# A decoder layer on one core: self scores from three fp32r products of parts, and cross keys and values ahead of the projections of x

## The reference

```
def reference(x, ctx_1024, mask, ...):
    x = x + self_attn(layernorm(x))                  # 16 heads of 64, softmax over queries (axis -2)
    x = x + cross_attn(layernorm(x), ctx_1024, mask)  # 16 heads of 8, 512 keys
    x = x + ffn(layernorm(x))                        # 8 experts, top 2, and a shared one
    return x

# self_attn
q, k, v = (split_heads(x @ W + b, 16) for W, b in ((Wq, bq), (Wk, bk), (Wv, bv)))
pattern = einsum('bhid,bhjd->bhij', k, q) / 8
prob = softmax(pattern, axis=-2)
out = einsum('bhis,bhid->bhsd', prob, v)
```

## Time and profile before

| | us |
|---|---|
| median of 3 runs | 206.96 |
| lowest and highest run | 206.8, 211.75 |
| profiled execution | 206.72 |
| its span, first to last instruction | 204.9 |
| PE busy in the span | 194.9 (95%) |
| DVE, ACT, POOL busy | 153.0, 132.2, 97.2 |

### The profile page before, as it was taken

One profiled execution on the slowest core, in us unless ns is written; L12 is line 12 of the kernel. 1 busy time (PEld: TensorE's weight loads), 2 busy tenths in 40 slices (PEclk: granted clock), 3 DMA queues, 4 the chain that ended last, 5 costly groups with the idle time before them and its releaser, 6 DMA issues.

```text
span 204.9 us, 4417 instructions
## 1 busy us (share of the span) xinstructions
PE 194.9 (95%) x1562; PEld 151.7 (74%) x1562; DVE 153.0 (75%) x409; ACT 132.2 (65%) x308; POOL 97.2 (47%) x145
## 2 busy tenths in 40 slices
PE   7899998999999899996999999999989999999995
PEld 7588876678777667863756656676658799999994
DVE  2576787577559788579999999999983867458844
ACT  2475458697679649279998898987985332462220
POOL 7599107757673787905759991002400017500330
PEclk9999999999999999999999999999999999999999
DMA  6970477989734402324004200000000000000001
GB/s 174 386 198 3 154 102 93 100 102 134 89 53 126 134 2 77 79 82 153 0 4 122 31 3 0 2 3 2 0 3 0 3 0 5 0 0 16 0 0 38
DMA packets 10980, 12.67 MB, mean 62 GB/s; under 512 B 984, under 2 KB 8920, under 8 KB 10888
## 3 DMA queue, kind: packets, MB, share of 16 engines
q1 hardware_dynamic: 9856, 11.15, 26.8%
q10 hardware_dynamic: 1008, 1.06, 1.6%
q0 software_dynamic: 96, 0.20, 0.6%
HBM read 10.96 MB, written 1.44 MB: 61 GB/s over the span
## 4 chain that ended last, share of the span: by engine, by line
PE 69%; DVE 10%; ACT 9%; issue 4%; POOL 3%; DMA 3%; ACTq 0%; DVEq 0%; POOLq 0%
PE ps L938 13%; PE ps L899 8%; PE ps L962 8%; PE ps L825 7%; PE ps L841 6%; PE ps L714 6%; PE ps L797 5%; PE ps L876 5%; PE ps L858 4%; ACT q_t L631 3%; PE ps L727 3%; DMA biases<-in_biases 3%; ACT prob L597 3%; PE ps L916 2%; DVE q_t L1164 2%
## 5 line engine op out<-in xcount | busy, mean ns | idle before, releaser
L1164 DVE CUSTOM_DVE_ANT_0 q_t<-ps,mask_add 128x512 f32<-128x512 f32 x64 | 41.3, 682 | 3.3 <-PE ps L858 2.0
L486 POOL TENSOR_TENSOR prob<-prob,rec 128x512 f32<-128x512 f32 x32 | 32.4, 1040 | 23.5 <-DVE rec L1223 23.5
L597 ACT ACTIVATE prob<-ps,low 128x256 f32<-128x256 f32 x64 | 29.7, 490 | 10.5 <-DVE low L1154 10.5
L631 ACT ACTIVATE q_t<-q_t,low 128x512 f32<-128x512 f32 x44 | 29.3, 717 | 4.2 <-DVE low L1164 4.1
L1154 DVE TENSOR_REDUCE low<-ps 128x2 f32<-128x512 f32 x32 | 20.4, 682 | 8.5 <-PE ps L797 8.5
L899 PEld LDWEIGHTS ps<-ident,q_t 128*128 128x128 f32 x176 | 19.6, 141 | 8.7 <-ACT q_t L631 2.9
L522 POOL TENSOR_TENSOR place_k<-place_k 128x256 f32<-128x256 f32 x10 | 7.3, 732 | 38.8 <-DVE place_k L1189 38.8
L899 PE MATMUL ps<-ident,q_t 128*128 128x128 f32 x176 | 23.7, 276 | 2.1 <-ACT place_k L667 0.8
L617 ACT ACTIVATE q_t<-ps 128x512 f32<-128x512 f32 x18 | 10.6, 598 | 21.1 <-PE ps L938 21.1
L1210 DVE TENSOR_TENSOR q_t<-q_t,ps 128x512 f32<-128x512 f32 x18 | 12.2, 684 | 11.8 <-PE ps L938 7.0
L841 PE MATMUL ps<-ident,prob 128*128 128x128 f32 x128 | 18.4, 278 | 1.4 <-POOL prob L486 0.9
(11 more groups left out here) (173 smaller groups left out, 428.9 us busy)
## 6 DMA issues: line engine op xcount, KB each, us to landing
k_stack<-k_dram SPq DMA_DIRECT2D x9, 256.0 KB
wg<-in_L_ffn_w_gate SPq DMA_DIRECT2D x1, 1024.0 KB, 23.6
wu<-in_L_ffn_w_up SPq DMA_DIRECT2D x1, 1024.0 KB, 35.0
q_stack<-q_dram SPq DMA_DIRECT2D x6, 144.0 KB
k_dram<-prob SPq DMA_DIRECT2D x1, 768.0 KB, 3.6
w_in<-in_L_attn_Wq ACTq DMA_DIRECT2D x2, 256.0 KB, 5.6
context<-in_ctx SPq DMA_DIRECT2D x1, 512.0 KB, 5.7
w_in<-in_L_attn_Wv SPq DMA_DIRECT2D x1, 512.0 KB, 7.5
```

Of the source, the lines that this page charges most:

```text
L486: nc.gpsimd.tensor_tensor(pr, pr, rec1[:, s % 2, r, :].unsqueeze(2).to_broadcast([P, C, S]), ALU.mult).then_inc(s_norm1, 1)
L597: e = nc.scalar.activation(prob1[:, s % 3, r, c * S:(c + 1) * S], ps[:, 2 * (s % 2) + r, c * S:(c + 1) * S], ACT.Exp, bias=low1[:, s % 2, ...
L631: nc.scalar.activation(prob2[n % 3][:, c, :], score2[n % 2][:, c, :], ACT.Exp, bias=low2[:, n % 2, c:c + 1], scale=-1.0).then_inc(s_exp2, 1)
L1164: nc.vector.tensor_tensor_reduce(out=score2[n % 2][:, c, :], in0=ps[:, 2 * (n % 2) + c, :], in1=mask_add[:, c, :], scale=1.0, scalar=3e38, ...
```

## The change

*Parts.* For each item of q and k ACT now writes the high part with its bias (fp32r, `q1_high`, `k1_high`, in the places of `q1_t` and `k1_t` and what follows), and DVE, after it, the low part from the same bank into `qk1_low`. The scale of -1/8 moves from the evacuation of q into the parts of Wq. The scores are three products for each head, with the two heads in turn. `qk1_low` lies where `k2_stack` will lie, which is why the loads of the stack now wait for the scores of their batch row and are made for one batch row at a time.

*Prologue.* Cross keys and values come first in the list of items, around the transposed x; transfers are issued in another order and the context in two halves; the mask moves into the first cycle; 12 matmuls on the identity stand at the start instead of 17.

```diff
-    out = [("x_t", 0, "dve"), ("kx", 0, "act"), ("kx", 1, "act")]
+    out = [("kx", 0, "act"), ("x_t", 0, "dve"), ("kx", 1, "act"), ("vx", 0, "act"), ("vx", 1, "act")]
     for p in range(NP):
-        out += [("q", p, "act"), ("k", p, "dve")]
-        if p == 2:
-            out += [("vx", 0, "act"), ("vx", 1, "act")]
+        out += [("q", p, "dve"), ("k", p, "dve")]
...
         @block.sync
             load(x_in[:, 0:C, :], a["x"][:, 0:C, :], d_x)
+            load(ctx_t[:, 0:BANK], a["ctx_1024"][:, 0:BANK], d_ctx[0])
             load(wk1[:, 0:BANK], a["L0_attn_Wk"][:, 0:BANK], d_qk[1][0])
-            load(ctx_t, a["ctx_1024"], d_ctx)
-            load(wk2[:, :], a["L0_xattn_Wk"], d_wk2)
             load(wv2[:, :], a["L0_xattn_Wv"], d_wv2)
+            load(wk1[:, BANK:2 * BANK], a["L0_attn_Wk"][:, BANK:2 * BANK], d_qk[1][1])
...
-            sp.wait_ge(d_kdram, 16)
-            for j in range(PARTS):
-                for i in range(PARTS):
-                    r = (j * PARTS + i) * HD2
-                    load(k2_stack[r:r + HD2, :, :], k2_dram[j].rearrange("(d h) t -> d h t", d=HD2), d_kstack)
+            def stack_keys(b):
+                sp.wait_ge(d_kdram, 16)
+                sp.wait_ge(s_score1, 2 * NP * (b + 1))
+                for j in range(PARTS):
+                    for i in range(PARTS):
+                        r = (j * PARTS + i) * HD2
+                        load(k2_stack[r:r + HD2, b, :, :],
+                             k2_dram[j, :, b * SK:(b + 1) * SK].rearrange("(d h) t -> d h t", d=HD2), d_kstack[b])
...
+            stack_keys(0)
             for b in range(B):
                 sp.wait_ge(s_qparts, b + 1)
...
                 if b == 0:
+                    stack_keys(1)
                     sp.wait_ge(s_pv1, N_SELF)
...
         @block.scalar
+            def high_parts(j, kind, which):
+                act.wait_ge(s_item, j + 1)
+                to, bias = (q1_high, bq1_s[:, which:which + 1]) if kind == "q" else (k1_high, bias1[:, 1, which:which + 1])
+                nc.scalar.activation(to[:, which, :], ps[:, j % 8, :], ACT.Identity, bias=bias).then_inc(s_hi1, 1)
...
         @block.tensor
+                for c in range(C):
+                    for part, (qi, ki) in enumerate(BIG_PARTS):
+                        for r in range(2):
+                            rows = slice(HD1 * r, HD1 * (r + 1))
+                            q = (q1_high[rows, p, b * S + c * P:b * S + (c + 1) * P],
+                                 qk1_low[rows, b, 0, p, c * P:(c + 1) * P])[qi]
+                            k = (k1_high[rows, p, b * S:(b + 1) * S], qk1_low[rows, b, 1, p, :])[ki]
+                            last = mm(ps[:, 2 * (s % 2) + r, c * S:(c + 1) * S], q, k,
+                                      start=part == 0, stop=part == len(BIG_PARTS) - 1)
+                            if c == C - 1 and part == len(BIG_PARTS) - 1:
+                                last.then_inc(s_score1, 1)
...
         @block.vector
+                nc.vector.scalar_tensor_tensor(out=qk_parts[:, i, 1, cols], in0=w[:, cols], scalar=(-SCALE1, 1.0)[i],
+                                               in1=qk_parts[:, i, 0, cols].bitcast(F32),
+                                               op0=ALU.mult, op1=ALU.subtract).then_inc(s_qkparts, 1)
...
-                    ins = nc.vector.tensor_scalar(k1_t[:, which, :], bank, bias1[:, 1, which:which + 1], None, ALU.add)
+                    dve.wait_ge(s_item, j + 1)
+                    dve.wait_ge(s_hi1, 2 * which + "qk".index(kind) + 1)
+                    ins = nc.vector.scalar_tensor_tensor(
+                        out=qk1_low[:, :, "qk".index(kind), which, :], in0=bank.rearrange("p (b t) -> p b t", b=B),
+                        scalar=bias, in1=high[:, which, :].rearrange("p (b t) -> p b t", b=B).bitcast(F32),
+                        op0=ALU.add, op1=ALU.subtract)
...
+                    if g == 0:
+                        dve.wait_ge(d_mask, 16)
+                        nc.vector.tensor_scalar(mask_add[:, :, :], mask_in, 0, MASKED, ALU.is_equal, ALU.mult
+                                                ).then_inc(s_maskadd, 1)
                     reciprocals1(g + 1)
```

111 lines of the change are left out of this document (55 added, 56 removed).

## The result

The changed kernel takes 208.12 us (median of six runs, 207.48 to 209.03); the kernel before, run beside it, 207.37 us. The ratio is 1.0048 with a 95% interval of 1.0025 to 1.0071. A second measurement of the same kernel, twelve runs, gave 208.16 us and 1.0042 [1.0013, 1.0070]. So the change costs about 0.5% where 205.9 us, about 0.5% less, was forecast: the sign is wrong and the time 2.2 us off, though inside the range of 203.3 to 208.4. Disturbed runs are left out of the ratios and not of the medians, so a median can stand above its ratio.

The account below looks back on a forecast made before the run. TensorE's sum and the chain through VectorE and ScalarE were taken to tie. 206.72 - 0.85 (scores) - 0.2 (prologue), mask and transfers 0, plus 0.24 for the median gave 205.9 us; own range 204.9 to 206.9, with rivals 203.3 to 208.4.

Parts of the forecast that it names:

- The scores: Self attention: pair 1.72 us instead of 2.03, cycle 6.8 instead of 6.97; 0.85 us gained over the pairs.
- The low parts: Prologue, VectorE: 16 low parts at 0.66 us in a row, 10.6 us, the last done at 25.4.
- I expect the same wait: Prologue: VectorE's last weight part again waits behind GpSimd's subtraction, ending at 14.6 to 15.0, say 14.8 us.
- the better case (both escape): Rival: VectorE's weight parts get ahead of GpSimd's subtraction; scores 1.2 us earlier, 204.7 us; chance 0.17.
- The rival that ended on the slower side: Prologue: low parts slow, 1.0 us each, 5.4 us more, 211.3 us; at half of that 208.6; chance 0.09.
- the prologue's gain of 0.2 us: VectorE's low parts eat the 1.7 us TensorE saves; first scores at 26.2 instead of 26.38 us.
- the part on transfers: Late transfers: key stack behind the FFN weights done by about 70, query stack issued at 79.39; cost 0.
- The start of the projections: Prologue, TensorE: q and k projections start at 10.4 to 10.9 us and are done by about 22.
- The first rival: Prologue: VectorE escapes GpSimd's subtraction and follows TensorE; scores at 25.0, 204.7 us; chance 0.17.
- this gap: Prologue: TensorE idle for about 1 us before the fourth chunk of values, which waits for its bank.
- The mask: Moved into the first cycle inside VectorE's wait; cost 0.2 us, offset by 0.16 from the earlier minimum, together 0.
- the milder slow low parts: Prologue: low parts slowed by half of the full slow case, giving 208.6 us; full case's chance 0.09.

Follow-up runs that it names:

- heads in turn: Changed kernel with all six score matmuls of one head ahead of the other's, instead of alternating: 209.51 us, ratio 1.0068 to the kernel before.
- scores alone: Changed kernel's fp32r scores and q/k parts, but item order, first transfers, warm-up and ScalarE's order of the kernel before: 206.65 us, ratio 0.9994 to the kernel before.
- transfers alone: Changed kernel with context in one piece, second on SyncE's queue, and first query weights ahead of the biases: 208.87 us, ratio 1.0051 to the kernel before.
- after again: Second measurement of the unmodified changed kernel, twelve runs: 208.16 us, ratio 1.0042 to the kernel before; its profile 207.23 us at full clock.
- old items, new transfers: Changed kernel with its transfers, but TensorE's items and ScalarE's order of the kernel before: 207.36 us, ratio 0.9983 to the kernel before.
- context half early: Changed kernel with the context's second half third instead of fifth on ScalarE's queue: 209.04 us, ratio 1.0115 to the kernel before.
- old transfers: Changed kernel with its item order, but the transfers of the kernel before (context in one piece, third on SyncE's queue): 210.81 us, ratio 1.0102 to the kernel before.
- ScalarE rounds first: Changed kernel with ScalarE's rounding of second weight halves ahead of the second context key's and values' evacuations: 207.62 us, ratio 0.9988 to the kernel before.
- after: The changed kernel in its first measurement: 208.12 us, ratio 1.0048 to the kernel before; its profile 209.03 us at mean clock 0.992.
- all but GpSimd's wait: The combined version without the line making GpSimd's value-weight split wait for VectorE's four weight parts: 206.75 us, ratio 0.9952 to the kernel before.
- GpSimd waits: Changed kernel with one line making GpSimd's value-weight split wait for VectorE's four weight parts: 206.32 us, ratio 0.9950 to the kernel before.
- the combined version: Changed kernel with context whole and early, query weights before biases, x first, ScalarE's rounding earlier, GpSimd's split waiting: 204.99 us, 0.9881 to before; again 205.71, 0.9931.
- the wait filled: Changed kernel with eight overwritten identity matmuls in TensorE's wait ahead of the fourth value chunk: 207.75 us, ratio 1.0019 to the kernel before.
- the prologue alone: Changed kernel's prologue, transfers and mask, but q and k evacuated in one step and fp32 scores as before: 207.37 us, ratio 1.0005 to the kernel before.

## Why the prediction was wrong

**The scores: right.** Pair 1.60 us (1.72 forecast), both halves together, the cycle 6.81 (6.8), the wait for VectorE's copy kept. Everything behind the first score gained 0.87 us (0.85). The order of the heads hardly matters for the overlap, as the run with the heads in turn shows. On this point the Trainium skill ("TensorE: Matmul & The Clock Gate", section "The mechanism" of its part 3) lists that weight loads overlap running matmuls only where the row group differs; the paragraph above that list also lets a load go ahead into a background weight buffer. The runs speak against the "only": with the heads in turn, one half alone takes a record with its own weight load 0.12 us after the last (50.43, 50.55), the same pace as with alternating halves.

**The low parts: right.** 0.66 us each in a row and 0.74 alone, as forecast, also beside GpSimd's passes. From the end of the last weight part to the first score it takes 11.49 us in five profiles in which the low parts follow at once, whenever they begin:

| profile | weight parts end | first scores | from there to the end |
|---|---|---|---|
| scores alone | 15.00 | 26.49 | 179.66 |
| transfers alone | 16.07 | 27.56 | 179.48 |
| after again | 16.20 | 27.69 | 179.54 |
| old items, new transfers | 16.31 | 27.80 | 179.48 |
| context half early | 17.97 | 29.46 | 179.53 |

Three more (old transfers, ScalarE rounds first, heads in turn) have 11.48 to 11.50, and after, whose clock falls just there, 11.64. The forecast had 25.4 + 0.8 - 14.8 = 11.4 for it.

**When they start: the step that failed.** The prediction took the end of the weight parts, 14.8 us, from the earlier trace rows, with the sentence "I expect the same wait". It came at 16.20 and 16.70. As the version with the scores alone shows with the same starts, the 3.49 us of the earlier trace rows are one part of 0.69 us that got ahead of the subtraction and one that was held for it. The prediction knew this row and made a rival of the better case (both escape); it did not see the worse one. In after both come behind: the first waits for the whole subtraction, the second then for GpSimd's next pass. The rival that ended on the slower side looked at the low parts, not at what stands ahead of them. So the term of the sum that failed is the prologue's gain of 0.2 us: it was a loss of 1.38. The Trainium skill ("SBUF — State Buffer", section "Who interferes with whom") states that a VectorE instruction with two SBUF inputs contends with a GpSimd instruction that reads SBUF, and that the one issued first holds the port for its whole length. The rows agree: 2.77 and 1.52 us beside GpSimd, 0.69 without, and no effect on the low parts, which read PSUM and one SBUF tile.

**Why they come behind.** The prediction wrote that ScalarE's rounding "should end at about the same time (11.6 to 12)". It ended at 12.98, and at 12.75 in after again. Two things stand one behind the other. The second half of Wq, now two places further back on ScalarE's queue, landed at 11.2 and 10.8, not at 8.4. And ScalarE came to it 0.6 to 0.8 us later still, because evacuations of a context key and of values had been put ahead, which waited for a context half that landed at 9.2 and 9.0. The sum had no term for the first transfers (the part on transfers dealt only with the late ones). The start of the projections, forecast at 10.4 to 10.9, was 11.73 to 11.95 for the same reason; that costs nothing here, since they end at 23.20 in after again and TensorE then waits 1.53 us for VectorE.

The runs share this out, though each score start is that of one execution. New transfers alone leave ScalarE's order as the limit and bring the scores 0.13 us forward; ScalarE's order alone leaves the transfer as the limit and brings some 0.5% of the time. Both together (with x turned first) bring 2.0 us of the start (27.69 to 25.70), GpSimd's wait alone some 2 us of the time, and all of it 2.4 us of the start (to 25.26). Either the parts come early or GpSimd lets them pass. The first rival's price was sound: with VectorE out of GpSimd's way and nothing late ahead of it, the combined version's profile has 204.83 us, where 204.7 was worked out.

**The clock: not in the sum.** Where VectorE is 1.5 to 1.8 us late, TensorE stands still just ahead of the first scores. Six of twelve runs have a lower mean clock and are 1.25 us longer, two of six in the first measurement. In the one of them that was profiled the first pair ran at 1.2 GHz and took 1.26 us more, and with the wait filled such runs were gone. By the profiles at full clock after is 0.51 us slower than before (1.38 - 0.87); a third to a half of the runs at 1.25 us more bring the rest of the measured 0.4 to 0.5%. The prediction expected this gap ("about 1 us") and gave it no price. The wait doesn't decide alone: with 1.53 us in after again and 1.84 us in the transfers alone the clock stayed at 1.00. Nor is it the only place: other versions' profiles show half clock from 12 us (GpSimd waits, behind 3.18 us of waiting for the context), from 71 us (all but GpSimd's wait), from 74 and 98 us (ScalarE rounds first) and from 98 us (old transfers).

**The mask and the range.** The mask cost 0.25 us with the prologue alone (0.2 forecast, though the rows give 33.93 - 33.17 = 0.76 us of overlap where the prediction wrote 0.6). The shorter scores gave it back: from the first scores to those of the first full cycle, after again takes 40.35 - 27.69 = 12.66 us, before 12.72. The range was said to take in the milder slow low parts, but these were priced at 208.6 us, above its end at 208.4; the measured 208.12 lies inside it for another reason.

**What stays open:** why the context half lands anywhere between 8.7 and 10.8 us with one and the same order of transfers, and the second half of Wq behind it between 10.7 and 14.8; and why the clock falls in some executions and not in others.

## What to carry to other kernels

A duration in a profile that contains a wait is worth only as much as the order that made it: before reusing the 3.49 us of two instructions, split them, see which one was held and by what, and ask which of them is held after the move. An early item in a queue is an item that everything behind it waits for: a step may go to the front only with the transfers that feed it, and these push back others. Where a side engine's long pass (here 3.7 us of GpSimd, needed 8 us later) can hold the engine that sets the pace, let it wait: that one line was worth 1% in the changed kernel, and nothing that could be shown once the parts came early.
